# Convolutions split into float32r matmuls in a fused convolution and quantized feed-forward kernel

## What is computed

```python
# 1. a causal convolution of each channel with its own 512 taps, plus a skip term
K = 2.0 * einsum('hn,hnl->hl', Ct, exp(P)).real        # taps from 64 modes per channel
y = irfft(rfft(u, n=2*L) * rfft(K, n=2*L))[..., :L] + u * D[:, None]
y = y * (arange(L)[None, :] < length[:, None])         # mask by the sample's length
# 2. a feed-forward layer over the last axis (512 -> 1376 -> 512), fp8-rounded inputs and weights
gate, up = fq(y, in_scale) @ gate_w.T, fq(y, in_scale) @ up_w.T
out = x + fq(silu(gate) * up, down_in_scale) @ down_w.T
```

## Time and profile before

| | |
|---|---|
| time, median of 3 runs | 321.7 us (321.67 to 321.93) |
| the profiled execution's own time | 321.68 us |
| its span | 319.9 us |
| TensorE, VectorE, ScalarE busy | 308.4, 187.3, 161.3 us |
| the blocks' slots begin (block 0's slot 2) | 37 us |
| block 1's slots begin | 59.8 us |

### The profile page before, as it was taken

The page is one execution under the profiler, slowest core; times in us unless marked ns, Lnnn a source line. Parts: engine busy times, 40 slices in busy tenths (PEclk is TensorE's granted clock), DMA queues, the critical chain, the costliest instruction groups (busy, mean ns, idle before and its releaser), DMA issues.

```text
span 319.9 us, 4409 instructions
## 1 busy us (share of the span) xinstructions
PE 308.4 (96%) x1561; PEld 162.0 (51%) x1587; DVE 187.3 (59%) x408; ACT 161.3 (50%) x222; POOL 13.7 (4%) x25
## 2 busy tenths in 40 slices
PE   1999999999999999999999999999999999999996
PEld 0467655554455554555455544555455554444443
DVE  6977588475637664465634756375744747433443
ACT  3924556364545364464635546453643646644550
POOL 3031000000001000000001000010001000010010
PEclk9999999999999999999999999999999999999999
DMA  6879999400005570078202680066500770070018
GB/s 200 190 190 230 275 321 328 164 1 2 0 0 101 161 264 2 0 131 299 96 0 36 164 326 0 0 110 235 182 0 0 134 262 0 2 132 0 0 22 243
DMA packets 14013, 38.40 MB, mean 120 GB/s; under 512 B 1470, under 2 KB 6558, under 8 KB 11052
## 3 DMA queue, kind: packets, MB, share of 16 engines
q1 hardware_dynamic: 8412, 26.61, 23.6%
q0 software_dynamic: 5584, 11.57, 20.8%
HBM read 33.93 MB, written 15.81 MB: 155 GB/s over the span
## 4 chain that ended last, share of the span: by engine, by line
PE 93%; DVE 3%; DMA 2%; issue 1%; DVEq 0%; SPq 0%
PE up_ps L588 23%; PE gate_ps L588 23%; PE y_ps L512 22%; PE down_ps L526 17%; PE down_ps L629 1%; PE down_ps L542 1%; PE y_ps L542 1%; PE y_ps L629 1%; DMA toep<-kpad_scratch 1%; DMA prm<-in_params 1%; PE down_ps L466 1%; PE gate_ps L554 1%; PE up_ps L554 1%; DMA kpad_scratch<-hq 1%; DVE xt L902 0%
## 5 line engine op out<-in xcount | busy, mean ns | idle before, releaser
L882 DVE SCALAR_TENSOR_TENSOR hv<-sil,fac,up_ps 128x512 f32<-128x512 f32 (+1 forms) x88 | 65.6, 746 | 116.5 <-PE up_ps L588 86.1
L413 ACT ACTIVATE sil<-gate_ps,fac 128x512 f32<-128x512 f32 (+1 forms) x88 | 60.4, 686 | 128.3 <-PE gate_ps L588 122.5
L588 PE MATMUL up_ps<-yq,wu 128*128 128x512 bf16 (+3 forms) x367 | 88.6, 363 | 0.3
L588 PE MATMUL gate_ps<-yq,wg 128*128 128x512 bf16 (+3 forms) x366 | 88.2, 363 | 0.6 <-DVE hv L882 0.3
L512 PE MATMUL y_ps<-xt,toep 128*128 128x512 f32 (+3 forms) x256 | 80.4, 434 | 0.2 <-DMA toep<-kpad_scratch 0.2
L526 PE MATMUL down_ps<-wd,hq 128*128 128x512 bf16 (+1 forms) x251 | 65.4, 379 | 0.7
L512 PEld LDWEIGHTS y_ps<-xt,toep 128*128 128x128 f32 x256 | 47.2, 190 | 21.5 <-issue 2.9
L588 PEld LDWEIGHTS gate_ps<-yq,wg 128*128 128x128 bf16 x372 | 36.2, 100 | 40.0 <-issue 1.7
L588 PEld LDWEIGHTS up_ps<-yq,wu 128*128 128x128 bf16 x372 | 36.3, 100 | 38.3
L394 ACT ACTIVATE hq<-hv 128x1024 uint16<-128x1024 uint16 (+1 forms) x48 | 46.8, 975 | 0.0
L526 PEld LDWEIGHTS down_ps<-wd,hq 128*128 128x128 bf16 (+1 forms) x264 | 25.9, 98 | 32.5 <-issue 12.6
(11 more groups left out here) (148 smaller groups left out, 99.8 us busy)
## 6 DMA issues: line engine op xcount, KB each, us to landing
xt<-in_xT SPq DMA_DIRECT2D x8, 1024.0 KB, 7.5
out<-in_x SPq DMA_DIRECT2D x7, 1024.0 KB, 5.7
out<-res POOLq DMA_DIRECT2D x7, 1024.0 KB, 7.8
toep<-kpad_scratch SPq DMA_DIRECT2D x6, 1024.0 KB, 10.0
toep<-kpad_scratch SPq DMA_DIRECT2D x8, 256.0 KB, 3.8
wd<-in_down POOLq DMA_DIRECT2D x1, 1280.0 KB, 22.3
xt<-in_x SPq DMA_DIRECT2D x1, 1024.0 KB, 7.4
out<-xt SPq DMA_DIRECT2D x3, 256.0 KB, 3.8
```

What stands on the lines that cost most here:

```text
L413: nc.scalar.activation(sil[b][0:w, :], gate_ps[b][0:w, :], ACT.Silu, scale=fac[0:w, S_GATE:S_GATE + 1]).then_inc(silu_done, 1)
L588: mm = nc.tensor.matmul(ps[b][0:w, cols], wt[:, k, c * P:c * P + w], yq[par][:, version, k, cols], start=(k == 0), stop=(k == LB - 1))
L882: v.scalar_tensor_tensor(hv[c // 2 % 3][0:w, c % 2], sil[b][0:w, :], fac[0:w, S_UP:S_UP + 1], up_ps[b][0:w, :], ALU.mult, ALU.mult).then_i ...
```

## The change

Beside each x tile and each taps tile stand now a high part and a low part in the type float32r (a float32 that TensorE reads in reduced precision). ScalarE copies x to the high part `xh`, with rounding, and VectorE subtracts it from x for the low part `xl`; the same for the first 384 columns of the taps (`th`, `tl`). Distances 0, 1 and 2 of a convolution are then three float32r matmuls, th*xh, th*xl and tl*xh, in place of one float32 matmul; distance 3 (128 columns) stays float32. This holds for 26 channels. The four channels of block 0 and the first two of block 1 stay as they were (`conv_whole`).

A tile of the split holds two channels (a pair), and there is one for each pair, so that the second half of block g + 2 can be split when block g + 1 has used it. `HIGH_PLAN` puts the copies of block g + 2 in slots 4 and 5 (pair 0) and 8 and 9 (pair 1) of block g, the subtractions in slots 5 and 6, and 9 and 10. For pair 1 of block 1 they stand in the ramp. Before the first piece of a channel TensorE waits for both subtractions of its pair instead of the loads.

SyncE's list is unrolled, and the loads of block g + 3 now stand ahead of the wait for the add of block g - 1. In the ramp the first two channels of block 1 come one `by_channel` later, and on ScalarE `copy_k(2)` comes behind the copies for block 1.

```diff
+SHORT = L - P
+        th = [sb(f"th{i}", [P, 2, SHORT], F32R) for i in range(2)]
+        tl = [sb(f"tl{i}", [P, 2, SHORT], F32R) for i in range(2)]
+        xh = [sb(f"xh{i}", [P, 2, L], F32R) for i in range(2)]
+        xl = [sb(f"xl{i}", [P, 2, L], F32R) for i in range(2)]
...
             load_toep(2, 0)
             copy_x(0, 0)
-            next_conv(3, 1)
-            copy_x(1, 1)
-            with sp.Fori(0, (NBLK - 4) // 2) as j:
-                for par in range(2):
-                    at_least(sp, added[par], 16 * (j + 1))
-                    copy_x(2 * j + 2 + par, par)
-                    next_conv(2 * j + 4 + par, par)
-            sp.wait_ge(added[0], 16 * (NBLK // 2 - 1))
-            copy_x(NBLK - 2, 0)
+            for g in range(NBLK - 2):
+                if g + 3 < NBLK:
+                    sp.wait_ge(y_ready, HB * (g + 2))
+                    load_x_t(g + 3, (g + 3) % 2)
+                    load_toep(g + 3, (g + 3) % 2)
+                if g:
+                    sp.wait_ge(added[(g - 1) % 2], 16 * ((g - 1) // 2 + 1))
+                copy_x(g + 1, (g + 1) % 2)
...
+            def high_x(g, par, half, pair):
+                at_least(act, xt_in[par], 16 * (half + 1))
+                at_least(act, y_ready, HB * (g - 1) + 2 * pair + 2)
+                nc.scalar.copy(xh[pair][:], xt[par][:, 2 * pair:2 * pair + 2]).then_inc(x_high, 1)
+            def high_taps(g, par, half, pair):
+                at_least(act, conv_in[par], 16 * half)
+                at_least(act, y_ready, HB * (g - 1) + 2 * pair + 2)
+                nc.scalar.copy(th[pair][:], toep[par][:, 2 * pair:2 * pair + 2, 0:SHORT]).then_inc(taps_high, 1)
...
                     if ahead and c in CODE_PLAN:
                         code_y(g + 1, 1 - par, CODE_PLAN[c])
+                    if ahead == 2 and c in HIGH_PLAN:
+                        high_x(g + 2, par, half + 1, HIGH_PLAN[c])
+                    if ahead == 2 and c - 1 in HIGH_PLAN:
+                        high_taps(g + 2, par, half + 1, HIGH_PLAN[c - 1])
...
-            for h in range(HB):
-                code_y(0, 0, h)
+            code_y(0, 0, 0)
+            code_y(0, 0, 1)
+            code_y(0, 0, 2)
+            high_x_first(1)
+            code_y(0, 0, 3)
+            high_taps_first(1)
             copy_k(2)
...
+            def conv(g, par, h, distances):
                 m = HB * g + h
+                pair, q = h // 2, h % 2
                 if distances[0] == 0:
+                    at_least(pe, x_split, 2 * (g - 1) + pair)
+                    at_least(pe, taps_split, 2 * (g - 1) + pair)
                     at_least(pe, yv_done, m - 1)
                 for d in distances:
+                    cols, rest = slice(d * P, (d + 1) * P), slice(0, L - d * P)
+                    if d == 3:
+                        nc.tensor.matmul(y_ps[q][:, 3 * P:L], toep[par][:, h, cols], xt[par][:, h, rest],
+                                         start=False, stop=False)
+                        continue
+                    for n, (taps, xs) in enumerate(((th, xh), (th, xl), (tl, xh))):
+                        last = nc.tensor.matmul(y_ps[q][:, d * P:L], taps[pair][:, q, cols], xs[pair][:, q, rest],
+                                                start=(d == 0 and n == 0), stop=(d == 2 and n == 2))
...
             by_channel(0)
-            conv(1, 1, 0, 0, [0, 1, 3, 2])
             by_channel(1)
-            conv(1, 1, 0, 1, [0, 1, 3, 2])
+            conv_whole(1, 0)
             by_channel(2)
+            conv_whole(1, 1)
             by_channel(3)
...
+            def low_x(g, pair):
+                at_least(dve, x_high, 2 * (g - 1) + pair)
+                v.tensor_tensor(xl[pair][:], xt[g % 2][:, 2 * pair:2 * pair + 2], xh[pair][:].bitcast(F32),
+                                ALU.subtract).then_inc(x_split, 1)
+            def low_taps(g, pair):
+                at_least(dve, taps_high, 2 * (g - 1) + pair)
+                v.tensor_tensor(tl[pair][:], toep[g % 2][:, 2 * pair:2 * pair + 2, 0:SHORT], th[pair][:].bitcast(F32),
+                                ALU.subtract).then_inc(taps_split, 1)
...
                     if ahead and c in FINISH_PLAN:
                         finish_y(g + 1, 1 - par, FINISH_PLAN[c])
+                    if ahead == 2 and c - 1 in HIGH_PLAN:
+                        low_x(g + 2, HIGH_PLAN[c - 1])
+                    if ahead == 2 and c - 2 in HIGH_PLAN:
+                        low_taps(g + 2, HIGH_PLAN[c - 2])
                     if c == CH - 1 and ahead == 2:
                         scale_y(g + 2, 0)
...
+            finish_y(0, 0, 3)
+            low_x(1, 1)
             scale_y(1, 0)
+            low_taps(1, 1)
...
+HIGH_PLAN = {4: 0, 8: 1}
```

More of the change, by code:

```diff
@@ L422, in slots, with high_x_first, high_taps_first @@
                         code_y(g + 1, 1 - par, CODE_PLAN[c])
+                    if ahead == 2 and c in HIGH_PLAN:
+                        high_x(g + 2, par, half + 1, HIGH_PLAN[c])
+                    if ahead == 2 and c - 1 in HIGH_PLAN:
+                        high_taps(g + 2, par, half + 1, HIGH_PLAN[c - 1])
                     if c == OUT_SLOTS[-1] and not first:
[L424 removed]
+                        down_scaled(g - 1, 1 - par, half - (1 - par), HB - 1)
             act.wait_ge(scales_ready, 1)
[L427 to L428 removed]
+            def high_x_first(pair):
+                act.wait_ge(xt_in[1], 16)
+                nc.scalar.copy(xh[pair][:], xt[1][:, 2 * pair:2 * pair + 2]).then_inc(x_high, 1)
+            def high_taps_first(pair):
+                act.wait_ge(toep_first[HB + 2 * pair], 16)
+                act.wait_ge(toep_first[HB + 2 * pair + 1], 16)
+                nc.scalar.copy(th[pair][:], toep[1][:, 2 * pair:2 * pair + 2, 0:SHORT]).then_inc(taps_high, 1)
+            code_y(0, 0, 0)
[4 more added lines that the diff above has]
+            high_taps_first(1)
             copy_k(2)
[L430 removed]
+            slots(0, 0, 0, True, 2)
             for stored_k in k_stored:
@@ L498, in _, with conv_whole @@
             warm(WARM[3])
-            def conv(g, par, half, h, distances):
+            def conv_whole(g, h):
+                pe.wait_ge(toep_first[HB * g + h], 16)
+                if h == 0:
+                    pe.wait_ge(xt_in[g], 16)
+                at_least(pe, yv_done, HB * g + h - 1)
+                for d in (0, 1, 3, 2):
+                    last = nc.tensor.matmul(y_ps[h % 2][:, d * P:L], toep[g][:, h, d * P:(d + 1) * P],
+                                            xt[g][:, h, 0:L - d * P], start=(d == 0), stop=(d == 2))
+                last.then_inc(y_ready, 1)
+            def conv(g, par, h, distances):
                 m = HB * g + h
+                pair, q = h // 2, h % 2
                 if distances[0] == 0:
[L504 to L509, removed]
+                    at_least(pe, x_split, 2 * (g - 1) + pair)
+                    at_least(pe, taps_split, 2 * (g - 1) + pair)
                     at_least(pe, yv_done, m - 1)
                 for d in distances:
-                    last = nc.tensor.matmul(y_ps[h % 2][:, d * P:L], toep[par][:, h, d * P:(d + 1) * P],
-                                            xt[par][:, h, 0:L - d * P], start=(d == 0), stop=(d == 2))
+                    cols, rest = slice(d * P, (d + 1) * P), slice(0, L - d * P)
[6 more added lines that the diff above has]
+                                                start=(d == 0 and n == 0), stop=(d == 2 and n == 2))
                 if d == 2:
@@ L557, in by_channel, with beside @@
                             mm.then_inc(ready, 1)
-            def beside(g, par, half, c, down, ahead):
+            def beside(g, par, c, down, ahead):
                 for step, h, distances in CONV_PLAN.get(c, ()):
                     if step <= ahead and (down or (step, h) != (1, 1)):
-                        conv(g + step, (par + step) % 2, half + (1 if step == 2 else par), h, distances)
+                        conv(g + step, (par + step) % 2, h, distances)
                 if down and not ahead:
@@ L567, in beside, with slots @@
                     down_part(g - 1, 1 - par, c)
-            def slots(g, par, half, down, ahead):
+            def slots(g, par, down, ahead):
                 for c in range(CH):
@@ L581, in slots @@
                             if c == 0 and hi == HB:
-                                beside(g, par, half, c, down, ahead)
+                                beside(g, par, c, down, ahead)
                             if c == 0:
@@ L592, in slots @@
                     if c or not down:
-                        beside(g, par, half, c, down, ahead)
+                        beside(g, par, c, down, ahead)
             for h in range(HB):
-                conv(0, 0, 0, h, [0, 1, 3, 2])
+                conv_whole(0, h)
             k_of(2)
@@ L610, in _ @@
             with pe.Fori(0, (NBLK - 4) // 2) as j:
[L611 to L615, removed]
+                slots(2 * j + 1, 1, True, 2)
```

(17 more changed lines are left out.)

14 lines of the change are left out of this document (6 added, 8 removed).

## The result

The changed kernel takes 325.8 us (325.51 to 326.09, 4 runs) against 321.8 us in the same session: 1.0124 times the time before, 95% interval 1.0107 to 1.0142. The forecast was 319.6 us, faster; it came out slower by 4.0 us, outside the range.

What follows compares the result with a forecast made beforehand. TensorE was taken to bound the kernel, busy 308.4 of 319.9 us. From 321.7 us, -12.3 + 3.8 + 0.2 + 5 x 1.22 = -2.1 gave 319.6 us, range 315 to 325.

Steps and rivals of the forecast that it cites:

- Part 1: Convolutions: float32r passes taken at the bf16 distance; a channel takes 1.68 us, 0.47 less, and 26 channels give 12.3 us.
- The forecast's own sign of being wrong: In the profile after: spacings above 0.12 us at 256 columns, or the gap released by something other than low_taps.
- Part 3: Slot 7, steady blocks: TensorE waits for VectorE's tap subtraction of slot 6, a stall of about 1.2 us, 1.22 charged.
- Part 4: Block 0, slot 7: TensorE is ready at 49.6, low_taps done at 53.0 to 53.2, a stall of 3.8 us.
- rival (d): Late taps or ScalarE copies, or a clock falling in block 0: one to two us each, 320.6 to 323; chance 0.17.
- Part 5: Moved copies and loads: copy_k(2) ends 1.8 us later, block 2's taps land at 47.9 instead of 46.1; all cost nothing.
- (a): The float32r weight load doesn't hide: 0.19 us per 256- or 384-column pass, 8.5 us more, 328; chance 0.13.
- (b): A float32r pass costs two columns' time per column, 0.43 us for 512: 37 us more, 354; chance 0.10.
- (c): Stall mostly gone, subtraction quicker or TensorE later: 313 for all of it, 316 for half; chance 0.12.

## Why the prediction was wrong

The mechanism was right and its largest term was sized wrong; with a forecast gain of 2.1 us left over from 12.3, that was enough to turn the sign. A clock that fell in block 0 added 1.6 us.

- **The price of a float32r pass (Part 1) is the step that failed most.** It was taken at the bf16 distance. It has 0.011 us more for each matmul, 2.6 us for 234 of them, and some more where the type changes (0.017 a pair in the row above). A channel saves 0.335 us and not 0.47, 26 channels 8.7 and not 12.3: 3.6 us of the 6.2 between forecast and result. The text itself had the point from which this decides, a load of 0.136 us at 256 columns, or 2.1 us over all; but it looked for a load that binds, at the short matmuls only. The measured excess is spread over all 234 matmuls and is no bound at all. A term whose rows are missing should have had an excess per instruction among its bounds: 234 x 0.009 us is the whole gain. The forecast's own sign of being wrong, spacings above 0.12 us at 256 columns, was too coarse for the same reason: 0.12 is what came.
- **The Trainium skill** ("TensorE: Matmul & The Clock Gate", Back-to-back issue gap) gives columns over 2.4 GHz plus 2.5 ns for what it calls an isolated matmul, and less, 131 ns at 512 columns, for a stream with weight loads. The bf16 rows here are such a stream and agree with the first (0.216 and 0.110), not with the second; float32r is 0.011 above the first. The Trainium skill ("FP8 and Floating Point Precision", TensorE Precision Notes) gives true float32 four passes and says nothing of the time of the reduced one. That it is one pass in four was the prediction's reading, and it holds nearly: the measured pass is 1.05 of a bf16 one at 512 columns and 1.09 at 256.
- **The wait in slot 7 (Part 3) was right** in its place, its releaser and its chain (6.31 us of VectorE for 6.33). It was 1.28 us (1.13 in the fifth block and in a written-out loop), and 0.10 for the load that was not made ahead, for the 1.22 charged: 0.7 us in five blocks. The prediction's own working comes to 122.73 - 121.45 = 1.28; it was charged as 1.22, which is 0.3 of the 0.7.
- **The wait in block 0 (Part 4) was right**, 3.6 us for 3.8. The length is in part luck: TensorE got there at 50.4 for 49.6 and low_taps ended at 53.9 for 53.0, both 0.8 to 0.9 us late. What failed is that the clock stood only among rival (d)'s small causes. It fell, and cost 1.6 us.
- **What is moved (Part 5)**: the taps of block 2 landed near 48.4, after ScalarE had waited 0.97 us for them, later than the 47.9 forecast, and cost nothing, as VectorE got to low_taps only at 52.9. The loads ahead of the adds never made anyone wait.
- **The rivals**: (a) gave the right side for a wrong reason (at 256 columns the distance is 0.12 and not the 0.19 of a load that doesn't hide). (b) and (c) are out: a pass of 512 columns takes 0.227 us and not 0.43, and VectorE's subtractions take 1.22 and 0.95 us, as forecast. (d) came true in the clock alone.
- Added up in the profile: 3.6 for the pass and 1.6 for the clock make 5.2, and the 0.7 of the steady waits less 0.2 in block 0 makes 5.7, of the 5.8 us by which the span missed 317.8.

## What to carry to other kernels

Where a change swaps a sure gain on the bounding engine for work on two others, write down one block of the helper engine's queue, instruction by instruction, up to the one that is waited for: the shares of busy time said that there was room for 4.3 us, and the wait was set by one slot that was already full. Put such work in the slot with the most room, at least one slot earlier than the last that could do; here one number in a plan was worth 7 us. And when a forecast gain is what is left of a large one, ask how small an excess per instruction, times their count, would eat it.

## What the runs showed that was not expected

- A float32r matmul costs 0.227, 0.17 and 0.120 us at 512, 384 and 256 columns, about 0.011 above bf16, with all other engines idle too. At 128 columns it costs 0.111, twice a bf16 one (four gate matmuls of 128 columns take 0.22 us in TensorE's timeline), and three of them more than one float32 matmul.
- After 3.6 us of idling TensorE's clock stood at 1.2 GHz for most of the next 3.9 us, with TensorE busy, and this cost 1.6 us. Twelve useless matmuls in the gap kept it at 2.4. The same kernel can have it or not: with a gap of 2.8 us the clock fell in four of five executions, with one of 3.4 us in two of four, and there the time ran from 332.0 us without it to 334.55 with the longest. With gaps of 1.3 us it never fell. (The gaps are those of the profiled executions.) So a median of such a kernel mixes both; the granted clock of each execution has to be read beside its time.
- A wait in TensorE's loop, where its count is computed, costs 0.15 us more than one outside, where it is a constant, if TensorE really waits there (1.28 against 1.13); in a kernel that doesn't wait, nothing (37.15 both). Whether the computed count or the loop costs it was not tried apart.
